# Scattering expert rows into four shared sums per token instead of one row per token and expert

## The reference

```python
combine = jnp.zeros((T, NUM_EXPERTS), dtype=x.dtype)
combine = combine.at[jnp.arange(T)[:, None], top_idx].set(top_w)
h1 = jax.nn.silu(jnp.einsum('th,eih->eti', x, w_gate))
h1w = h1 * combine.T[:, :, None]
routed = jnp.einsum('eti,ehi->th', h1w, w_down)
shared = jax.nn.silu(x @ w_gate_shared.T) @ w_down_shared.T
return (routed + shared).reshape(B, S, H)
...
x = _layernorm(x + _L0_ffn_ref(x, ...), axis=-1)
```

## Time and profile before

| | us |
|---|---|
| median of three timed executions | 1122.86 |
| lowest and highest of them | 1120.07, 1125.76 |
| span of the profiled execution | 1222.8 |
| PE busy | 998.1 (82%) |
| DVE busy | 849.7 (69%) |
| POOL busy | 745.4 (61%) |
| ACT busy | 634.9 (52%) |

### The profile page before, as it was taken

The page is one execution under the profiler, slowest core; times in us unless marked ns, Lnnn a source line. Parts: engine busy times, 40 slices in busy tenths (PEclk is TensorE's granted clock), DMA queues, the critical chain, the costliest instruction groups (busy, mean ns, idle before and its releaser), DMA issues. The chain is left out here.

```text
span 1222.8 us, 17645 instructions
## 1 busy us (share of the span) xinstructions
PE 998.1 (82%) x4918; PEld 825.6 (68%) x4918; DVE 849.7 (69%) x1645; ACT 634.9 (52%) x1565; POOL 745.4 (61%) x648
## 2 busy tenths in 40 slices
PE   6499989999999999898798862378888787787476
PEld 5377777888878878787587752266666666666364
DVE  0689999999999999999999456244444434444266
ACT  5685766857758668477464340144444434443300
POOL 0464747576789788978898545456655555555400
PEclk9899999999999999999899995699999889888789
DMA  7384817541241421511411112778867767775497
GB/s 241 132 267 145 278 45 255 171 155 40 59 140 60 136 87 40 183 57 62 140 60 46 67 70 92 213 232 236 243 200 220 218 191 229 212 214 182 134 375 264
DMA packets 118462, 195.49 MB, mean 160 GB/s; under 512 B 17684, under 2 KB 83378, under 8 KB 115922
## 3 DMA queue, kind: packets, MB, share of 16 engines
q1 hardware_dynamic: 79890, 134.54, 35.9%
q0 software_dynamic: 16512, 35.19, 8.0%
q10 hardware_dynamic: 21952, 24.51, 6.2%
HBM read 155.21 MB, written 75.64 MB: 189 GB/s over the span
## 5 line engine op out<-in xcount | busy, mean ns | idle before, releaser
L449 POOL TENSOR_TENSOR inf_all<-bc_all,du 128x1024 f32<-128x1024 f32 x128 | 300.5, 2364 | 101.5 <-DVEq L1652 52.0
L2201 POOL DMA_INDIRECT yp_dram<-u,sz x216 | 212.6, 984 | 167.0 <-issue 83.8
L1654 DVE TENSOR_TENSOR_SCAN DA<-DA,inf_all 128x1024 f32<-128x1024 f32 x128 | 293.1, 2290 | 15.4 <-ACT DA L712 12.5
L1106 PE MATMUL Y<-hb_all,ident 128*128 128x256 f32 x1024 | 244.5, 386 | 21.8 <-DVE u L1670 20.4
L1106 PEld LDWEIGHTS Y<-hb_all,ident 128*128 128x128 f32 x1024 | 194.9, 193 | 53.8 <-DVE u L1670 24.6
L712 ACT ACTIVATE DA<-dl,a_neg 128x255 f32<-128x255 f32 x512 | 211.9, 461 | 0.2
L2229 PE MATMUL DA<-sz,hb_all 128*128 128x128 f32 x864 | 150.7, 301 | 41.4 <-issue 27.6
L2236 PE MATMUL DA<-hb_all,sz 128*128 128x256 f32 x432 | 147.6, 426 | 32.6 <-issue 23.3
L2229 PEld LDWEIGHTS DA<-sz,hb_all 128*128 128x128 f32 x864 | 125.3, 209 | 56.3 <-issue 35.6
L1661 DVE TENSOR_TENSOR hb_all<-DA,bc_all 128x1024 f32<-128x1024 f32 x128 | 156.0, 1219 | 7.9 <-DVE DA L1654 0.5
L2261 ACT ACTIVATE sz<-DA 128x128 f32<-128x128 f32 x216 | 59.8, 277 | 166.4 <-PE DA L2229 87.1
(11 more groups left out here) (453 smaller groups left out, 1619.9 us busy)
## 6 DMA issues: line engine op xcount, KB each, us to landing
hb_all<-in_w_moe SPq DMA_DIRECT2D x216, 256.0 KB
bc_all<-bc_dram SPq DMA_DIRECT2D x32, 1024.0 KB, 5.6
inf_all<-xe_dram SPq DMA_DIRECT2D x216, 140.0 KB
bc_all<-yp_dram SPq DMA_DIRECT2D x16, 1024.0 KB, 6.0
xe_dram<-zeros ACTq DMA_DIRECT2D x2, 7420.0 KB, 25.7
xe_dram<-zeros ACTq DMA_DIRECT2D x1, 7560.0 KB, 27.4
yp_dram<-u,sz POOLq DMA_INDIRECT x216
xt<-in_xT SPq DMA_DIRECT2D x8, 256.0 KB
```

The lines of the kernel that those rows point to most:

```text
L449: g.tensor_tensor(inf[(b * NTAU + t) % NI][:, :, :], bc[gr][:, 0, :, :], du[p][:, c, :].unsqueeze(1).to_broadcast([P, SG, T]), ALU.mult).t ...
L1106: ins = mm(Y[:, 0:T], ident[:, :], hb[t % NH][:, n, :], start=gr == 0 and n == 0, stop=gr == NG - 1 and n == SG - 1, skip_group_check=True)
L1654: v.tensor_tensor_scan(da[:, :], da[:, :], inf[(b * NTAU + t) % NI][:, :, :].rearrange("p n t -> p (n t)"), 0.0, ALU.mult, ALU.add).then_i ...
L2201: g.indirect_dma_start(yp_dram, bass.IndirectOffsetOnAxis(ap=pid[:, half * UNROLL + s_:half * UNROLL + s_ + 1], axis=0), ys[s_][:, :], Non ...
```

## The change

`yp_dram` (eight rows per token) and `acc_dram` (one) become one tensor `ya_dram` with `NA` = 4 rows per token. Row 0 of a token gets the shared expert's output from SP, as `acc_dram` did; rows 1 to 3 are cleared by three transfers from ACT in turn 3 of the front. In the expert stage the scatter of the block in place s_ of its turn adds its rows to row s_ mod 4 of each token, with an accumulating DMA. Two DMAs that add to the same row must not overlap, so POOL waits, ahead of each scatter, until the one four blocks earlier has landed; and ahead of the first until the clears and the last store of the shared output have. The constant that gives the destinations now names the token (times 4) and not the choice.

The combine loads four rows per token, two tiles to a transfer of 1 MB, eight tiles ahead. VectorE folds row 1 onto row 0, TensorE adds rows 2, 3 and the fold; rows 2 and 3 no longer wait for the fold. There are four PSUM banks, four output tiles, and a store covers two tiles.

The diff, without renamed constants and most unchanged lines:

```diff
@@ -58,6 +58,7 @@
 LIFT = 1 << 18
+NA = 4
...
@@ -91,10 +92,9 @@
-        acc_dram = nc.dram_tensor("acc_dram", (NT, D), FP32, kind="Internal").ap()
...
         xe_dram = nc.dram_tensor("xe_dram", (ROWS_X, XW), I32, kind="Internal").ap()
-        yp_dram = nc.dram_tensor("yp_dram", (NT * TOPK, D), FP32, kind="Internal").ap()
+        ya_dram = nc.dram_tensor("ya_dram", (NT, NA, D), FP32, kind="Internal").ap()
...
@@ -371,7 +371,7 @@
             def acc_store(b):
...
                 sp.sem_inc(tick, 1)
-                sp.dma_start(acc_dram[bass.ts(b, T), :].rearrange("(q p) d -> p q d", p=P), acc[:, :, :]).then_inc(acc_st.sem, 16)
+                sp.dma_start(ya_dram[bass.ts(b, T), 0, :].rearrange("(q p) d -> p q d", p=P), acc[:, :, :]).then_inc(acc_st.sem, 16)
...
@@ -426,7 +426,7 @@
             g.memset(one_f[:, :], 1.0).then_inc(k_pool.sem, 1)
-            g.iota(pairs_i, pattern=[[P * TOPK, NTILE], [1, TOPK]], base=0, channel_multiplier=TOPK).then_inc(k_pool.sem, 1)
+            g.iota(tokens_i, pattern=[[P * NA, NTILE], [0, TOPK]], base=0, channel_multiplier=NA).then_inc(k_pool.sem, 1)
...
@@ -781,6 +781,11 @@
             def clear_rest():
...
                 s.dma_start(rows_, zeros[:, :].bitcast(I32).unsqueeze(1).to_broadcast([P, NOVER, XW])).then_inc(blank.sem, 16)
+            def clear_sums():
+                rows_ = ya_dram.rearrange("(i p) a d -> p i a d", p=P)
+                for j in range(1, NA):
+                    s.dma_start(rows_[:, :, j, :], zeros[:, 0:D].unsqueeze(1).to_broadcast([P, NTILE, D])).then_inc(blank.sem, 16)
...
@@ -868,6 +873,8 @@
                     clear_rest()
+                if s == 3:
+                    clear_sums()
...
@@ -1760,7 +1767,7 @@
                 w8 = QT * TOPK
-                v.tensor_copy(rows_[:, :, P0:], pairs[:, bass.ds(b * w8, w8)].rearrange("p (q k) -> p q k", q=QT)).then_inc(pick.sem, 1)
+                v.tensor_copy(rows_[:, :, P0:], tokens[:, bass.ds(b * w8, w8)].rearrange("p (q k) -> p q k", q=QT)).then_inc(pick.sem, 1)
...
@@ -2193,13 +2200,22 @@
         def experts_gpsimd(pool):
...
             last = last_filled(pool)
+            by_row = ya_dram.rearrange("t a d -> (t a) d")
             def scatter(i, s_, half):
+                i_before, s_before = back(i, s_, NA)
+                if i_before >= 0:
+                    pool.wait_ge(y_sc[s_before].sem, y_sc[s_before].at(i_before, 16))
+                    pool.sem_inc(tick, 1)
...
                 pool.sem_inc(tick, 1)
-                g.indirect_dma_start(yp_dram, bass.IndirectOffsetOnAxis(ap=pid[:, half * UNROLL + s_:half * UNROLL + s_ + 1], axis=0), ys[s_][:, :], None,
-                                     bounds_check=NT * TOPK - 1, oob_is_err=False).then_inc(y_sc[s_].sem, 16)
+                g.indirect_dma_start(by_row, bass.IndirectOffsetOnAxis(ap=pid[:, half * UNROLL + s_:half * UNROLL + s_ + 1], axis=0), ys[s_][:, :], None, element_offset=s_ % NA * D,
+                                     bounds_check=(NT - 1) * NA, oob_is_err=False, compute_op=ALU.add).then_inc(y_sc[s_].sem, 16)
+            pool.wait_ge(blank.sem, blank.at(4 + NA - 1, 0))
+            pool.wait_ge(acc_st.sem, acc_st.at(NB - 1, 16))
+            pool.sem_inc(tick, 1)
...
@@ -2396,53 +2412,52 @@
-        y_in = [sig(f"y_in{i}", 32) for i in range(NY)]
+        y_in = [sig(f"y_in{i}", 16) for i in range(NY)]
...
         var_d, std_d, rstd_d, fin_d = sig("var_d"), sig("std_d"), sig("rstd_d"), sig("fin_d")
-        half = TOPK // 2 * D
-        Y8 = [bc_flat[:, i * TOPK * D:(i + 1) * TOPK * D] for i in range(NY)]
-        ac = [inf_flat[:, i * D:(i + 1) * D] for i in range(NY)]
-        ot = [inf_flat[:, (NY + i) * D:(NY + i + 1) * D] for i in range(2)]
+        YA = [bc_flat[:, i * NA * D:(i + 1) * NA * D] for i in range(2 * NY)]
+        ot = [inf_flat[:, i * D:(i + 1) * D] for i in range(4)]
         bs, bm, vr, sd, rd = [[sz_flat[1][:, n * 16 + i * 8:n * 16 + i * 8 + w] for i in range(2)] for n, w in enumerate((6, 2, 1, 1, 1))]
-        S = [PB, QA, QF]
+        S = [PB, QA, QF, Y]
         def combine_sync(sp, last):
-            sp.wait_ge(acc_st.sem, acc_st.at(NB - 1, 16))
...
-            def load(t):
-                i = t % NY
-                if t >= NY:
-                    sp.wait_ge(sum_f.sem, sum_f.at(t - NY, 1))
-                sp.dma_start(Y8[i][:, :], yp_dram[t * P * TOPK:(t + 1) * P * TOPK, :].rearrange("(p k) d -> p (k d)", p=P)).then_inc(y_in[i].sem, 16)
-                sp.dma_start(ac[i][:, :], acc_dram[t * P:(t + 1) * P, :]).then_inc(y_in[i].sem, 16)
-            for t in range(NY):
-                load(t)
-            for t in range(NTILE):
-                if t + NY < NTILE:
-                    load(t + NY)
-                sp.wait_ge(fin_d.sem, fin_d.at(t, 1))
-                sp.dma_start(out[t * P:(t + 1) * P, :], ot[t % 2][:, :]).then_inc(out_st[t % 2].sem, 16)
+            def load(h):
+                i = h % NY
+                if h >= NY:
+                    sp.wait_ge(sum_f.sem, sum_f.at(2 * (h - NY) + 1, 1))
+                sp.dma_start(bc_flat[:, 2 * i * NA * D:2 * (i + 1) * NA * D].rearrange("p (q c) -> p q c", q=2),
+                             ya_dram[2 * h * P:2 * (h + 1) * P, :, :].rearrange("(q p) a d -> p q (a d)", p=P)).then_inc(y_in[i].sem, 16)
+            for h in range(NY):
+                load(h)
+            for h in range(NTILE // 2):
+                if h + NY < NTILE // 2:
+                    load(h + NY)
+                sp.wait_ge(fin_d.sem, fin_d.at(2 * h + 1, 1))
+                at = 2 * (h % 2) * D
+                sp.dma_start(out[2 * h * P:2 * (h + 1) * P, :].rearrange("(q p) d -> p q d", p=P),
+                             inf_flat[:, at:at + 2 * D].rearrange("p (q d) -> p q d", q=2)).then_inc(out_st[h % 2].sem, 16)
             for i in range(2):
-                sp.wait_ge(out_st[i].sem, out_st[i].at(NTILE // 2 - 1, 16))
+                sp.wait_ge(out_st[i].sem, out_st[i].at(NTILE // 4 - 1, 16))
         def combine_tensor(pe):
             for t in range(NTILE):
-                i = t % NY
-                pe.wait_ge(fold_d.sem, fold_d.at(t, 1))
-                pe.wait_ge(y_in[i].sem, y_in[i].at(t // NY, 32))
+                i = t % (2 * NY)
...
                     pe.wait_ge(fin_d.sem, fin_d.at(t - len(S), 1))
+                pe.wait_ge(y_in[i // 2].sem, y_in[i // 2].at(t // (2 * NY), 16))
                 bank = S[t % len(S)]
-                for k in range(TOPK // 2):
-                    nc.tensor.matmul(bank[:, 0:D], ident[:, :], Y8[i][:, k * D:(k + 1) * D], start=k == 0, stop=False)
-                nc.tensor.matmul(bank[:, 0:D], ident[:, :], ac[i][:, :], start=False, stop=True).then_inc(sum_f.sem, 1)
+                for k in range(2, NA):
+                    nc.tensor.matmul(bank[:, 0:D], ident[:, :], YA[i][:, k * D:(k + 1) * D], start=k == 2, stop=False)
+                pe.wait_ge(fold_d.sem, fold_d.at(t, 1))
+                nc.tensor.matmul(bank[:, 0:D], ident[:, :], YA[i][:, 0:D], start=False, stop=True).then_inc(sum_f.sem, 1)
...
@@ -2455,9 +2470,9 @@
             def fold(t):
-                i = t % NY
-                dve.wait_ge(y_in[i].sem, y_in[i].at(t // NY, 32))
-                v.tensor_tensor(Y8[i][:, 0:half], Y8[i][:, 0:half], Y8[i][:, half:], ALU.add).then_inc(fold_d.sem, 1)
+                i = t % (2 * NY)
+                dve.wait_ge(y_in[i // 2].sem, y_in[i // 2].at(t // (2 * NY), 16))
+                v.tensor_tensor(YA[i][:, 0:D], YA[i][:, 0:D], YA[i][:, D:2 * D], ALU.add).then_inc(fold_d.sem, 1)
...
@@ -2475,9 +2490,9 @@
                 dve.wait_ge(rstd_d.sem, rstd_d.at(t, 1))
-                if t >= 2:
-                    dve.wait_ge(out_st[q].sem, out_st[q].at(t // 2 - 1, 16))
-                v.tensor_scalar(ot[q][:, :], S[t % len(S)][:, 0:D], bm[q][:, 0:1], rd[q][:, 0:1], ALU.subtract, ALU.mult).then_inc(fin_d.sem, 1)
+                if t >= 4:
+                    dve.wait_ge(out_st[t // 2 % 2].sem, out_st[t // 2 % 2].at(t // 4 - 1, 16))
+                v.tensor_scalar(ot[t % 4][:, :], S[t % len(S)][:, 0:D], bm[q][:, 0:1], rd[q][:, 0:1], ALU.subtract, ALU.mult).then_inc(fin_d.sem, 1)
```

More of the change, by code:

```diff
@@ L129, in decoder_kernel @@
         ones = sb("ones", [P, P], BF16)
-        pairs = sb("pairs", [P, NTILE * TOPK])
+        tokens = sb("tokens", [P, NTILE * TOPK])
         home = sb("home", [P, NE])
@@ L254, in decoder_kernel @@
         iota_i = [cum[:, q, :].bitcast(I32) for q in range(2)]
-        pairs_i = key[:, 0, 0:NTILE * TOPK].bitcast(I32)
+        tokens_i = key[:, 0, 0:NTILE * TOPK].bitcast(I32)
         top = sb("top", [P, QT, TOPK])
@@ L1625, in front_vector @@
             v.tensor_copy(slot0[:, :], iota_i[1]).then_inc(k_conv.sem, 1)
-            v.tensor_copy(pairs[:, :], pairs_i).then_inc(k_conv.sem, 1)
+            v.tensor_copy(tokens[:, :], tokens_i).then_inc(k_conv.sem, 1)
             dve.wait_ge(k_conv.sem, 3)
```

## The result

The changed kernel takes 1226.97 us (1223.49 to 1228.54), against 1121.46 us for the kernel before on the same chip: ratio 1.0939, 95% interval 1.0897 to 1.0981. It is 105.5 us slower, where 25.8 us less was forecast.

A forecast was written before the change was run, and what follows sets the result against it. The prediction took TensorE to bound the expert stage and loads the combine. Combine -26.8 us and last scatter +1 gave -25.8, so 1122.86 became 1097 us, with a range from 1089 to 1165.

The forecast's parts named there:

- (b): Expert stage, POOL's scatter instruction: 984 ns, 1.29 us with the gap to the next, taken as not growing; cost nothing.
- a slack of 0.41 us: Expert stage: POOL has 0.41 us a block left between its 1.29 us and the traced pace of 1.70.
- TensorE is the engine that is full: Expert stage: reason for costing the add's extra traffic at nothing, with DMA rising from 0.70 to 0.83.
- POOL becomes the bound: Rival, chance 0.22: in the expert stage the adding scatter grows by 0.49 us; with 0.2 of slack, 1160 us.
- 0.98 us more: Expert stage: POOL's scatter grows by 0.98 us if the read side doubles; at the traced slack +123 us, 1220.
- (a): Expert stage: each scatter waits for the landing four blocks earlier; 5 us taken, under 6.8, so it costs nothing.
- 5.0 at a pace of 1.24: Rival that the wait binds, chance 0.10: decides from landings of 6.8 us, or 5.0 at that pace; 1179 us.
- (c): Expert stage: the add's second read brings about 47 us of DMA time, costed at nothing; last scatter 1 us later.
- The combine: Last stage: shrinks from 66.6 to 39.8 us with four rows per token, 26.8 us less.
- The front: Clears from ACT's queue in turn 3: between 0 and 2.9 us, taken as 0, with VectorE's 98% as cover.

The follow-up runs named there:

- e0: The kernel before, unchanged, profiled a second time: 1117.24 us.
- e6: The kernel before with its scatters in four forms in turn, overwriting or adding 128 or 64 rows, for GpSimd's instruction times; no total time is given.
- e4: The kernel before plus only the wait, ahead of each scatter, for the landing of the scatter four blocks earlier: 1146.48 us, ratio 1.0228.
- e1: The changed kernel with its scatters overwriting instead of adding, all else kept: 1125.26 us, ratio 1.0037 to the kernel before.
- e8: The kernel before plus DRAM-to-DRAM copies of 512 rows of 1 KB from ACT's queue in the first 16 of 27 turns: 1122.97 us, ratio 1.0013.
- e5: The kernel before plus only three clears of 2 MB in turn 3, on a tensor nothing else uses: 1127.87 us, ratio 1.0069.
- e7: The kernel before with its eight rows in bf16 and a combine summing them on TensorE, two tiles a load: 1095.63 us, ratio 0.9780.

## Why the prediction was wrong

**The step that failed** is (b) of the scatters. It has two terms, POOL's 1.29 us a block, taken as unchanged, and a slack of 0.41 us, and both were wrong. "Whether the accumulating form takes longer to write out no row shows ... I take nothing": it takes 0.574 us more. (The reason given, 984 against 960 ns, compares two forms that overwrite and says nothing of one that adds.) "In the traced stage 0.41 us a block is left": nothing is left. Neither alone makes the loss that was measured: with a slack of 0.41 the growth is 0.16 us a block, 35 us, enough to use up the gain and little more, and with none but no growth it is nothing; measured are 123.7.

The slack was a mean, (1154.10 - 788.54) / 215 = 1.70 us, of an execution that was known to be 99.9 us too long. The prediction wrote down the right case, "none if the 99.9 us that the timed executions are shorter lie in this stage", then built the sum on the other. That trace held the answer: its scatters start 1.29 us apart in the median, and 122 of 215 stand right behind the one before (the earlier trace rows is one of them), so the mean of 1.70 was GpSimd's pace plus interruptions. The other 93 have 88.4 us of idle time beyond the usual 0.30, all that this stage was longer by than e0's, and 89 of them start 0.84 us after ACT's result: there ACT came late, and its largest wait is for TensorE's first product (87.1 us, 26.2 in e0), at a granted clock of 0.91 where e0's stage has 0.98. What made them late stays open. With the slack, "TensorE is the engine that is full", the reason for costing traffic and growth at nothing, failed too: in e0's stage ACT waits 85.2 us for POOL's scatters, and TensorE for ACT (18.7 us ahead of the second product).

**POOL becomes the bound** was the right rival, with 0.22. Its growth, 0.49 us, is near the 0.574; its time, 1160, was too low since it kept 0.2 us of slack. With none, and the growth that was measured, the same working gives 216 x 0.574 = 124, less the combine's gain, some 98 us more. Its reason, three entries for two, isn't borne out: e6's surcharge hardly goes by rows.

The Trainium skill (GPSIMD Engine Reference, When to use GPSIMD) has one core of a pair write a DMA's reads and the other its writes; the prediction took from it 0.98 us more, on the read side doubling. The trace agrees in direction only: 1558 ns is 1.58 times 984, and e6 shows why a doubling of row entries was the wrong unit.

**(a) The wait**: right for this kernel to within 1 us, by luck of the longer pace. By the semaphore events landings have a median of 4.6 us from POOL's start (5 was taken), and the latest is 7.3. With the 0.97 us of e4 the limit is 4 x 1.87 - 0.97 = 6.5, and that latest one makes the one longer gap, at 793.18: the profile names ACT there, but ACT's result is 7.4 us old and the landing 0.95. At the pace of before the same wait costs 25 us (e4), a bill that the longer instruction covers. The prediction's "5.0 at a pace of 1.24" had such a threshold, though without the 0.97 us, and by the pace it should have been priced.

**(c) The traffic**: under-sized, and right to cost nothing. The scatters' queue by the DMA view of the stage (packets, MB, share of 16 engines), in e0 and after:

```profile
q0 software_dynamic: 10272, 16.80, 16.6%
```

```profile
q0 software_dynamic: 30822, 16.85, 33.1%
```

The packets are three times as many, and 16.6% of 278 us became 33.1% of 402: 46 and 133 us, 87 more where 47 were expected. The Trainium skill (Collectives: The Full Stack, The bandwidth ceiling) puts an in-transfer add at two source reads for a write, from which came half the throughput; the trace agrees that it is dearer, and shows about a third of the throughput. The second read itself shows in no view: the queue's bytes stay 16.8 MB, and the changed kernel and e1, which overwrites the same rows, have the same HBM bytes (the changed kernel first):

```profile
HBM read 144.73 MB, written 81.93 MB: 186 GB/s over the span
```

```profile
HBM read 144.73 MB, written 81.93 MB: 202 GB/s over the span
```

What differs is the size of the packets in the trace: in e0 4054 of them hold 4096 bytes, four rows each, and in after every one of the 16,384 rows has its own of 1024 bytes, with 11264 more of 8 bytes. By e8 such a surplus costs nothing beside GpSimd's pace.

**The combine**: right. From its first load to the end it takes 1221.6 - 1181.5 = 40.1 us where 39.8 was forecast. A row of SyncE's timeline and two of VectorE's give its parts:

```profile
1181.52 2.11 SPq L2435 DMA_DIRECT2D bc_all<-ya_dram  x4
...
1186.41 0.76 DVE L2475 TENSOR_TENSOR bc_all<-bc_all 128x256 f32<-128x256 f32 x2 [22.59 <-DMA bc_all<-ya_dram]
...
1218.39 0.54 DVE L2495 TENSOR_SCALAR inf_all<-Y,sz 128x256 f32<-128x256 f32 x1
```

The load is there after 4.9 us (5.5), the fold takes 0.41 us (0.42), and only the first fold waits for a load. The store ends 2.7 us after the last result (2.3). Against e0 the gain from the last scatter on is 23.7 us; 25.8 was forecast, against a combine 2 us longer (and e4's was 6.8 longer).

**The front**: 0 was taken, with 2.9 as bound; it is 6.1 us in the profile and 7.7 in e5. The bound came from what the earlier clears, most of them larger, cost POOL and VectorE as traffic. The cost is another: ACT is held while it issues, and VectorE's 98% was no cover, because its scans take ACT's output.

By the measured terms the change is +123.7 in the stage, +6.1 in the front and -23.7 behind it.

## What to carry to other kernels

Before a stage is given slack, look at how often its engine's instructions stand back to back, and compare the median of their distances with the mean; a profile that is much longer than the timed executions has means that can't be carried over. An engine at 77% can be full, if its idle time is the same small gap before every instruction. Count what a change adds per instruction on such an engine first, since there it comes out in full, and what it saves elsewhere has to be larger than that.

## What the runs showed of the hardware

- An indirect scatter of 128 rows takes GpSimd 984 ns when it overwrites (1045 in e6) and 1558 when it adds (1560 in e6); 64 rows take 955 and 1419 in e6, and rows of 512 bytes 983 in e7. The price goes by the instruction, hardly by rows or bytes.
- An adding scatter moves its 16.8 MB in three times the packets, with 2.9 times the DMA engine time (133 us for 46): one of 1 KB for each row, where the overwriting one has mostly 4 KB for four.
- A scatter that waits for a landing starts 0.97 us after it (38 of 41 such gaps in e4, 35 of 40 in e1), and the profile's releaser names ACT or VectorE in most of them.
- DMA engines that are full (1.05 by packets, 377 GB/s) did not slow a stage that GpSimd paces (1.0013).
- Clears of 2 MB in rows of 1 KB, three in a row from ACT's queue, took 0.38, 1.97 and 7.05 us to issue (e5), and ACT's own work waited.
